# Gated cross attention and a quantised feed-forward layer: scores ahead of the value product in each step, and a context split in two halves

## The reference

```python
def _L0_xattn_ref(q, k, v, Wq, Wk, Wv, Wo, bo, mask):
    ...
    qh = split_heads(q @ Wq)
    kh = split_heads(k @ Wk)
    vh = split_heads(v @ Wv)
    dots = jnp.einsum('bhid,bhjd->bhij', qh, kh) * SCALE
    ...
    attn = jax.nn.softmax(dots, axis=-1)
    out = jnp.einsum('bhij,bhjd->bhid', attn, vh)
    out = out.transpose(0, 2, 1, 3).reshape(b, n, h * d)
    return out @ Wo + bo
x = x + jnp.tanh(g_xattn[0]) * _L0_xattn_ref(_layernorm(x, axis=-1), ctx_1024, ctx_1024, L0_xattn_Wq, L0_xattn_Wk, L0_xattn_Wv, L0_xattn_Wo, L0_xattn_bo, mask_BxS2_bf0)
x = x + jnp.tanh(g_ffn[0]) * _L0_ffn_ref(_layernorm(x, axis=-1), L0_ffn_w_gate, L0_ffn_w_up, L0_ffn_w_down)
```

## Time and profile before

| | |
|---|---|
| median of 3 runs | 1652.94 us (1652.37 to 1656.29) |
| profiled execution | 1651.4 us |
| its span, first to last instruction | 1649.5 us |
| mean granted clock | 0.985 of full speed |
| busy: PE, PE weight load, DVE, ACT, POOL | 93%, 76%, 84%, 76%, 64% |

### The profile page before, as it was taken

How to read it: one execution, slowest core, us unless ns; L and a number is a source line. 1 busy time by engine, 2 the same in 40 slices (tenths; PEclk the granted TensorE clock), 3 DMA queues, 4 the chain that set the end, 5 groups by cost and what they waited for, 6 DMA issues and landing times. The chain is left out here.

```text
span 1649.5 us, 38042 instructions
## 1 busy us (share of the span) xinstructions
PE 1535.6 (93%) x12556; PEld 1247.8 (76%) x12556; DVE 1379.2 (84%) x2231; ACT 1252.1 (76%) x3222; POOL 1048.6 (64%) x1004
## 2 busy tenths in 40 slices
PE   7899999999999999999999999889997997996998
PEld 5687877877877778778777787667775775775887
DVE  7887878888878788888888888868887998998996
ACT  6777877878777778777777777747667998896664
POOL 4988988888889888888888887900004775560000
PEclk9999999999999999999999999999998999997999
DMA  6554444444544454444444443549985885665664
GB/s 196 112 126 96 107 94 124 97 100 99 124 97 107 98 120 104 91 100 117 104 102 106 113 102 62 117 134 333 325 292 208 280 283 185 242 248 188 216 221 147
DMA packets 347365, 252.23 MB, mean 153 GB/s; under 512 B 287792, under 2 KB 317616, under 8 KB 344368
## 3 DMA queue, kind: packets, MB, share of 16 engines
q1 hardware_dynamic: 347312, 251.58, 54.0%
HBM read 105.25 MB, written 76.02 MB: 110 GB/s over the span
## 5 line engine op out<-in xcount | busy, mean ns | idle before, releaser
L496 ACT ACTIVATE prob<-masked,neg_max 128x128 f32<-128x128 f32 x1024 | 397.6, 391 | 59.3 <-DVE neg_max L664 57.2
L431 POOL TENSOR_TENSOR prob_parts<-prob,prob_parts 128x512 f16<-128x512 f32 x254 | 318.2, 1272 | 4.5 <-ACT prob_parts L504 4.5
L426 POOL TENSOR_TENSOR prob<-prob,scaled 128x512 f32<-128x512 f32 x256 | 271.4, 1060 | 20.1
L662 DVE TENSOR_TENSOR masked<-score,mask_add 128x512 f32<-128x512 f32 x256 | 174.4, 681 | 67.9 <-PE score L964 67.9
L504 ACT ACTIVATE prob_parts<-prob 128x512 f16<-128x512 f32 x254 | 159.2, 627 | 62.6 <-POOL prob L426 60.2
L496 ACT ACTIVATION_READ_ACCUMULATOR prob<-masked,neg_max 128x1 f32 x1024 | 193.6, 189 | 0.0
L664 DVE TENSOR_REDUCE neg_max<-masked 128x4 f32<-128x512 f32 x256 | 175.7, 686 | 8.8
L438 POOL TENSOR_TENSOR probT<-turn 128x512 f32<-128x512 f16 x125 | 179.9, 1439 | 0.0
L1724 POOL TENSOR_SCALAR xThi<-n_x 128x1024 fp32r<-128x1024 int16 x15 | 44.9, 2990 | 201.9 <-DMA n_x<-n_x_d 166.8
L977 PE MATMUL y<-wo_hi,o_hi 128*128 128x256 f32 x508 | 148.1, 292 | 9.8 <-DVE o_lo L669 9.2
L424 POOL TENSOR_TENSOR scaled<-rsums,pscale 128x4 f32<-128x4 f32 x256 | 65.1, 254 | 136.3 <-DVE rsums L656 136.1
(11 more groups left out here) (249 smaller groups left out, 4471.8 us busy)
## 6 DMA issues: line engine op xcount, KB each, us to landing
gate<-gate_d SPq DMA_DIRECT2D x30, 768.0 KB, 4.2
n_x<-n_x_d SPq DMA_DIRECT2D x25, 512.0 KB, 5.0
gate_d<-stage SPq DMA_DIRECT2D x8, 1536.0 KB, 5.5
n_u_d<-w_raw SPq DMA_DIRECT2D x16, 768.0 KB, 4.1
stage<-n_u_d SPq DMA_DIRECT2D x16, 768.0 KB, 6.1
gate_d<-gate SPq DMA_DIRECT2D x7, 1536.0 KB, 5.5
x_in<-in_x SPq DMA_DIRECT2D x16, 512.0 KB, 4.0
ctx_in<-in_ctx_columns SPq DMA_DIRECT2D x16, 512.0 KB, 4.7
```

Of the source, the lines that this page charges most:

```text
L426: gp.tensor_tensor(prob[:, h], prob[:, h], scaled[:, h, :].rearrange("p (b o) -> p b o", o=1).broadcast_to([P, NB, P]), ALU.mult).then_inc ...
L431: gp.tensor_tensor(prob_parts[:, h, 1], prob[:, h].rearrange("p b k -> p (b k)"), prob_parts[:, h, 0], ALU.subtract).then_inc(prob_low, 1)
L496: nc.scalar.activation(prob[:, h, b, :], masked[:, h, b, :], ACT.Exp, bias=neg_max[:, h, b:b + 1], accum_out=psums[:, h, b:b + 1]).then_in ...
L662: nc.vector.tensor_tensor(masked[:, h], score[h][:], mask_add[:], ALU.add).then_inc(masked_done, 1)
```

## The change

Four edits in `attention`:

1. On PE, `scores_free` and `scores` come ahead of `times_v`, with a `nop` that takes the waits; `times_v` has no waits of the scores inside any more.
2. On DVE, `ctx_low_part` writes one block k of the context at a time, between and behind the two `low` of x. It stands ahead of the last reciprocals of the step then. PE waits for each half where it needs it; SP's wait counts the halves.
3. On ACT in step 7, `copy_k` comes ahead of the first `high`, and `ctx_high_part` between the two `high`, ahead of the exponentials of half 1.
4. On ACT from step 3 on, the copy of the values comes ahead of the high part of the probabilities of half 0.

```diff
@@ sync
-                sp.wait_ge(ctx_split, g)
+                sp.wait_ge(ctx_split, KC * g)
@@ scalar, step
-                if nxt:
-                    high(g, *ts[0])
                 if new:
                     copy_k(g, c, u)
                 if nxt:
+                    high(g, *ts[0])
+                    ctx_high_part(g + 1)
                     high(g, *ts[1])
                 if soft:
                     exps(u - 1, 1)
-                if nxt:
-                    ctx_high_part(g + 1)
                 if isinstance(g, int) and g == 0 and c < 3:
                     w_high_part(4 + c)
-                if soft:
-                    high_prob(u - 1, 0, c % 2, NC // 2 * g + c // 2)
                 if new and c > 2:
                     for i, n in jobs_of(c, "v"):
                         b, before = nth(g, i)
                         act.wait_ge(projected[b], before + 1)
                         nc.scalar.activation(v_sb[:, n % NB, VH:2 * VH], proj[b][:], ACT.Copy).then_inc(copied[b], 1)
+                if soft:
+                    high_prob(u - 1, 0, c % 2, NC // 2 * g + c // 2)
@@ vector
-            def ctx_low_part(g):
-                dve.wait_ge(high_done, (KC + 1) * (g + 1))
-                nc.vector.tensor_tensor(t_lo[1][:], ctx_in[:], t_hi[1][:].bitcast(F32), ALU.subtract).then_inc(ctx_split, 1)
+            def ctx_low_part(g, k):
+                dve.wait_ge(high_done, (KC + 1) * g + (2 if not isinstance(g, int) or g > 0 else KC + 1))
+                nc.vector.tensor_tensor(t_lo[1][:, k], ctx_in[:, k], t_hi[1][:, k].bitcast(F32), ALU.subtract).then_inc(ctx_split, 1)
@@ vector, step
                 if nxt:
-                    for n in range(KC):
-                        low(g, *ts[n], (KC + 1) * (g + 1) + n)
+                    low(g, *ts[0], (KC + 1) * (g + 1))
+                    ctx_low_part(g + 1, 0)
+                    low(g, *ts[1], (KC + 1) * (g + 1) + 2)
+                    ctx_low_part(g + 1, 1)
...
-                if nxt:
-                    ctx_low_part(g + 1)
@@ tensor
                 def part_split(k):
-                    if n == 1 and k == 0:
-                        pe.wait_ge(ctx_split, g + 1)
+                    if n == 1:
+                        pe.wait_ge(ctx_split, KC * g + k + 1)
@@ tensor, step
+                if new:
+                    scores_free(g, c, u)
+                    pe.nop(nofuse=True)
+                    scores(g, c, u)
                 if old:
-                    times_v(u - 3, co, (g, c, u) if new else None)
-                if new:
-                    if not old:
-                        scores_free(g, c, u)
-                    scores(g, c, u)
+                    times_v(u - 3, co)
```

More of the change, by code:

```diff
@@ L829, in _ @@
                 low(-1, first_job(n), n, n)
-            ctx_low_part(0)
+            for k in range(KC):
+                ctx_low_part(0, k)
             w_low_part(2)
```

## The result

| | before | after |
|---|---|---|
| median (runs) | 1654.14 us (4, 1652.37 to 1656.29) | 1628.01 us (4, 1626.37 to 1631.1) |
| profiled execution, its span | 1651.4, 1649.5 us | 1627.69, 1625.9 us |

The ratio is 0.9844, with a 95% interval of 0.9823 to 0.9864: faster by 26 us, where 38 were forecast.

A forecast was written before the change was run, and what follows sets the result against it. PE bounds the steady steps and waits for ACT and DVE at the group's end. 15 × 2.36 = 35.4 plus 2.6 for edges takes 38.0 us off 1651.4: 1613.4, median 1.5 above, so 1615; range 1602 to 1636.

The forecast's parts named there:

- part of the gain lost: Case for the whole kernel's time: 1622 to 1645 us, chance 0.27.
- Edits 2 and 3, up to the halves: Group's end: context's low part in halves of 0.82 us on DVE, both ready before PE's key projection asks for them.
- The 1.47 gap: At the group's end PE waited 1.47 us until DVE had made the context's low part; claimed to close.
- `masked` "at about 603.85": Group's end on DVE: `masked` starts at about 603.85 instead of 606.21, so `o_lo` ends at 605.85.
- `kT` about 0.7 us earlier: ACT, step 7: `kT` ends at about 600.0 instead of 600.72, by 0.48 from its new order and 0.25 from edit 4.
- The 0.25 from edit 4: ACT, step 6: the values' copy fills part of a 1.85 us wait for POOL; what follows comes 0.25 us earlier.
- Edit 1 at zero ± 0.05 per step: PE's steady steps: changes of shape between neighbours sum to zero, ± 0.05 us in 125 steps, ± 6 us; no gain.
- the slower rival: Waits between value projection and scores cost PE time in every step; at 0.52 us in 125 steps, 1680 us; chance 0.05.
- The edges: Groups 0 and 15: 0.8 us from scores run in a `probT` wait, about 1 from edit 4, 0.8 at the end; together 2.6.
- half the gain stays: Rival: DVE or POOL late again at the group's end; 24 us gained, 1629, or 1641 with step losses; case chance 0.27.
- Its bound of 1.4 us: Lower bound of gain per change of group, with each context half held up by a POOL instruction for up to 1.0 us.
- PE takes all: Rival: `o_lo` in time, low parts 0.6 us a half, 2.86 us gained per change of group; 1607 us, chance 0.14.

The follow-up runs named there:

- the loop written out: Changed kernel with DVE's loop over groups 1 to 14 written out: 1618.67 us; edits 2 and 3 alone with that and ACT's tanh behind the first copies: 1614.02 us.
- its two experiments: Values copied ahead of the high part, alone on the kernel before: 1651.6 us, ratio 0.9989; changed kernel with that copy put back: 1628.57 us, ratio 0.9849.
- the early tanh: ACT's gate tanh, waiting for a DMA, in its old place ahead of the first step; changed kernel with it behind the first `kT` copy: 1626.37 us, 0.9834.
- the second run with the context in one piece: Repeat of the changed kernel with one 128x1024 subtraction for the context's low part, DVE's loop still in it: 1627.89 us, ratio 0.9839.

## Why the prediction was right in kind, and 13 us off

The forecast was 1615, the range 1602 to 1636; 1628.01 lies in the case "part of the gain lost". One of the 13 us is the kernel before, 1654.14 in these runs and 1652.94 in the forecast; 12 are gain that didn't come. By its own steps, on the group followed above:

- **Edits 2 and 3, up to the halves: right.** The gain comes from them alone (the experiment gives 0.9825). The second half was to end 8.87 us behind the start of step 7's query projection; the changed kernel gives 8.96. The halves took 0.84 and 0.67 us, forecast 0.82 each. The 1.47 gap closed.
- **`masked` "at about 603.85", right behind the low part: this step failed.** I took the DVE chain as "made of measured pieces", and left out the piece between two of them: the turn of DVE's loop, 0.45 us [0.45 <-issue]. In the trace before it can't be seen: what stood last ahead of the turn was the context's low part, 1.71 us long, and `masked` follows it without idle time. Edit 2 moved that instruction up and left the reciprocals, 0.18 us, as the last. From the query projection to the product with Wo I had 3.4 us and measured 3.68 (592.99 to 596.67); with the loop written out it is 3.13. Without the turn the halves would have beaten the forecast by 0.27; with it they missed it by 0.28.
- **`kT` about 0.7 us earlier: mis-sized.** It had two terms. The 0.48 for standing ahead of a `tx_hi` copy is right: with edits 2 and 3 alone step 6 to 7 fell from 8.33 to 7.82 or 7.84. The 0.25 from edit 4 came to nothing: its two experiments show no gain, and the new 0.31 us wait for the bank of `qT` stands where it would be. Its reason failed: what ends ACT's waits in step 6 is POOL, and the copy moved ahead of them didn't make POOL earlier.
- **Edit 1 at zero ± 0.05 per step: right in PE's stream** (7.63 stays, four more waits cost nothing; the slower rival is out), wrong in its effect on DVE: 0.11 us in step 4 to 5 and 0.14 in 6 to 7. I wrote "No gain, since PE is the bound" and did not ask what an earlier DVE would collide with.
- **Sum.** 0.28 + 0.25 + 0.11 + 0.14 = 0.78 us; the period misses its forecast by 0.76. Times 15 these are the 12 us. The edges were about right: group 0 took 65.38 us from scores to scores instead of 68.54, 3.16 less, of which 1.60 is its change of group; the last group's seven steps took 53.53 instead of 54.37. That makes 2.4, forecast 2.6. The start of the profiled execution, 3.2 us later, was no term of the forecast; how much of it is in the medians, and whether the edits have a part in it, is open.
- **The rival "half the gain stays"** has the right size and the wrong mechanism: it had each half of the context held up by POOL. The halves were hardly held, the first for 0.17 us more than the second took (0.84 and 0.67). DVE was late again through the turn, and in step 4 through two operations of 4 columns. That 1628 lies beside its 1629 is luck. Its bound of 1.4 us isn't what it says either: by the forecast's own times 1.4 stands for 1.0 us of delay in all, and 1.0 for each half would have left 0.36.
- **"PE takes all"**, 1607, is what the loop written out reaches at best, 1607.21 in one execution, 1614 in the median.

What stays open: whether the split of the context pays once the turn is gone (in one piece the reciprocals come 1.19 us into the query projection of step 0, in halves 0.99, so an estimate from these two times is up to 0.2 us per group), which share of groups is held in executions that weren't profiled, and why the first scores came later in all seven profiles with edits 2 and 3 and the early tanh. A scores-first kernel without the nop was not tried.

## What to carry to other kernels

Before a long instruction is moved away from the end of a loop, ask what it covered on its own engine: the turn of DVE's loop cost nothing behind 1.71 us of work and 0.5 us per group behind 0.18, where it shows as "issue". Ask where an engine that gets its input earlier will meet another; here more than half of the waiting that DVE saved went into its own collisions with POOL. And list the steps of a period one by one ahead of predicting: the 0.30 us above the ordinary step in step 4 stood in the trace before, beside a gap of 1.47 that drew the eye, and with its sequel in step 6 it was worth 0.7 us per group.

## Not expected of the hardware

- An operation of 128x4 elements on DVE took 0.16 us or 1.03, by whether it began less than 25 or more than 28 ns behind a POOL instruction of 128x512. One program has both kinds of groups in one execution, 62.8 and 63.55 us.
- A turn of a loop on DVE showed 0.45 us of idle behind a 0.18 us instruction, 0.25 us when a 1.22 us instruction stood ahead of that one, and none behind an instruction of 1.71 us.
- DVE's additions of two SBUF tensors of 128x512 (`probT`), started while a POOL instruction ran, ended 0.55 to 0.60 us behind it, in each of 97 cases; with one input in PSUM (`masked`, `o_lo`) they took 0.67 to 0.70 us whatever POOL did.
- In the changed kernel PE was granted half its clock from 16.8 to 23.5 us, from within a wait of 2.83 us on. The length of the wait doesn't tell: behind one of 1.71 us, in the kernel before, the clock stayed at 1.00, and so it did behind one of 2.78 us at the same place, in the second run with the context in one piece.
